# Step order, start and last layer of a seven-layer transformer kernel written as software-pipelined slots

## Time and profile before

| | us |
|---|---|
| three runs | 1559.39, 1562.4, 1566.7 |
| median | 1562.4 |
| the profiled execution's own time | 1564.65 |
| its span in the profile | 1562.9 |
| busy PE / DVE / ACT / POOL in the span | 1311.8 / 892.1 / 893.2 / 354.4 |
| granted TensorE clock, mean | 0.965 |

### The profile page before, as it was taken

The page is one execution under the profiler, slowest core; times in us unless marked ns, Lnnn a source line. Parts: engine busy times, 40 slices in busy tenths (PEclk is TensorE's granted clock), DMA queues, the critical chain, the costliest instruction groups (busy, mean ns, idle before and its releaser), DMA issues.

```text
span 1562.9 us, 66101 instructions
## 1 busy us (share of the span) xinstructions
PE 1311.8 (84%) x29736; PEld 750.4 (48%) x29736; DVE 892.1 (57%) x1825; ACT 893.2 (57%) x1535; POOL 354.4 (23%) x569
## 2 busy tenths in 40 slices
PE   2678889888998888888898988888879888989875
PEld 1344555455555545555554555544534333525333
DVE  3554556554556554555655555554577767787434
ACT  1255666566665666666666666655635565454720
POOL 3123222122223222222221222212211101020212
PEclk8699999999999999999999999999999999999987
DMA  8443344334244333434333434433223222110000
GB/s 164 97 96 83 86 96 91 80 64 95 75 93 110 78 60 84 105 77 98 89 82 70 89 82 88 94 89 51 75 64 59 58 45 61 17 32 4 10 2 15
DMA packets 133775, 113.69 MB, mean 73 GB/s; under 512 B 42360, under 2 KB 121054, under 8 KB 133086
## 3 DMA queue, kind: packets, MB, share of 16 engines
q1 hardware_dynamic: 133494, 109.47, 31.8%
HBM read 62.17 MB, written 47.25 MB: 70 GB/s over the span
## 4 chain that ended last, share of the span: by engine, by line
PE 39%; issue 26%; DVE 18%; POOL 8%; ACT 6%; DMA 3%; SPq 1%; POOLq 0%; DVEq 0%; ACTq 0%
PE pD L742 16%; PE pT L742 7%; PE pV L818 7%; DVE MX L1195 6%; PE pS L759 6%; DVE DEN L1413 4%; PE pD L943 3%; POOL RS L1525 2%; ACT PT L1098 1%; DVE R L1429 1%; ACT SQ L1113 1%; DVE CC L1266 1%; POOL VS L1604 1%; ACT XS L1151 1%; DVE DEN L1406 1%
## 5 line engine op out<-in xcount | busy, mean ns | idle before, releaser
L1098 ACT ACTIVATE PT<-pT 128x512 f32<-128x512 f32 x1088 | 622.6, 596 | 470.3 <-PE pT L742 460.8
L1195 DVE TENSOR_REDUCE MX<-pS 128x1 f32<-128x512 f32 (+4 forms) x928 | 500.2, 573 | 439.5 <-PE pS L759 435.1
L742 PE MATMUL pT<-Qop,Kop 128*32 128x256 bf16 (+2 forms) x7040 | 440.0, 300 | 29.8 <-ACT PT L1098 16.4
L759 PE MATMUL pS<-Kop,Qop 128*32 128x128 bf16 (+4 forms) x7168 | 316.6, 259 | 60.6 <-DVE MX L1195 27.2
L818 PE MATMUL pV<-PT,Vp 128*32 128x256 f32 (+2 forms) x3584 | 315.7, 434 | 5.8 <-ACT PT L1098 5.2
L759 PEld LDWEIGHTS pS<-Kop,Qop 128*32 128x32 bf16 x7168 | 182.0, 98 | 227.0 <-issue 120.7
L742 PEld LDWEIGHTS pT<-Qop,Kop 128*32 128x32 bf16 x7040 | 183.6, 97 | 165.7 <-issue 81.3
L818 PEld LDWEIGHTS pV<-PT,Vp 128*32 128x32 f32 x3584 | 125.2, 110 | 75.1 <-issue 23.1
L1525 POOL TENSOR_TENSOR RS<-VAR,MHALF 128x4 f32<-128x4 f32 x60 | 60.6, 1011 | 415.4 <-DVE VAR L1273 415.4
L1572 POOL TENSOR_TENSOR ATT<-NUM,DEN 128x512 f32<-128x512 f32 x28 | 35.6, 1273 | 407.0 <-DVE DEN L1413 407.0
L742 PE MATMUL pD<-HIDT,W 128*32 128x512 f32 x768 | 104.9, 599 | 0.0
(11 more groups left out here) (178 smaller groups left out, 1385.9 us busy)
## 6 DMA issues: line engine op xcount, KB each, us to landing
Qop<-Qs SPq DMA_DIRECT2D x56, 384.0 KB
Kop<-Ks SPq DMA_DIRECT2D x56, 384.0 KB
Qs<-XS SPq DMA_DIRECT2D x28, 384.0 KB, 2.7
Ks<-XS SPq DMA_DIRECT2D x28, 384.0 KB, 2.9
Qs<-XS SPq DMA_DIRECT2D x28, 256.0 KB, 3.0
Ks<-XS SPq DMA_DIRECT2D x28, 256.0 KB, 3.2
EM<-Es SPq DMA_DIRECT2D x24, 256.0 KB, 3.2
Ms<-MROW SPq DMA_DIRECT2D x336, 4.0 KB, 1.5
```

The costliest lines, as they stand in the source:

```text
L742: ins = matmul(dst[c:min(c + 32, cols)], lhs[:, c:min(c + 32, cols)], rhs, start=start, stop=stop, tile_position=(0, c))
L759: ins = matmul(pS[32 * c:32 * c + 32, k % 2, at:at + w], Qop[:, it.par, h, R * qb:R * (qb + 1)], Kop[:, it.par, h, :] if qb == 0 or it.ful ...
L1098: ac.activation(dst, exp_bank(it, k), ACT.Exp, scale=SCALE).then_inc(t_used, 1)
L1195: ins = ve.tensor_reduce(MX[:, u, g2, qbs[0]:qbs[-1] + 1:step], pS[:, k % 2, at:at + w * len(qbs)].rearrange("p (h n) -> p h n", n=w), axi ...
```

## The change

- Start: x of batch 0, the identity and the position term have a semaphore of their own (x0_in). PE transposes batch 0, then the bias rows, then multiplies Q and K of item 0, and then transposes the others (in pS and pT banks). Q and K of item 1 are multiplied before slot -1 begins. The loads of LOWM, NMQ, SEL, TRI, Wo, W2 and W1 move behind the places of item 1 in SP's slot -1, and are waited for at slot 0.
- EXM moves from step 3 to the start of step 2 on ACT.
- Preparations: centre_wo at step 2 (from 9), DP at PE step 3 and DVE step 4 (from 13 and 14) in pD bank 1 (from bank 0), AP at PE step 3 and DVE step 4 (from 8).
- Full items 25 to 27 ("direct"): no NUM and DEN copies; the reciprocals read PSUM, and DVE multiplies ATT at step 11.
- Halved banks: in items 24 to 26 for every expert product, in item 27 for the odd ones, DVE adds the second half of YE to the first and PE gathers with two products of the identity in place of four.
- Fused closing: DVE computes (x - mean) * G2, then times RS plus H1; POOL adds BE2 to H1 beforehand (residual). NMEAN goes; EPS is added on DVE. The second to last item's closing in the drain stands at steps 12, 16, 28, 30 (from 12, 16, 21, 23).

```diff
-LAST_CLOSE_STEPS = (12, 16, 21, 23)
+LAST_CLOSE_STEPS = (12, 16, 28, 30)
-CONSTS = 7
+CONSTS = 3
+        def direct(it):
+            return it.t > NMASKED
+        def halved(it, i):
+            return it.t < NITEMS - 1 or i % 2 == 1
...
-                + one("DEN", Z is not None, den_done, lambda: Z.t + 1)
+                + one("DEN", Z is not None, rec_done if Z is not None and direct(Z) else den_done, lambda: Z.t + 1)
                 + one("K", A is not None, r1_done, lambda: A.t * 2 + 2)
-                + one("DP", Z is not None and Z.b == 0, dp_done, lambda: Z.l + 1)
...
                 rnd(T, 2)
-                + one("NUM", Z is not None and Z.t < NITEMS - 1, num_done, lambda: Z.t + 1)
+                + one("DP", Z is not None and Z.b == 0, dp_done, lambda: Z.l + 1)
                 + one("AP", A is not None and A.b == 0 and after_norm(A.l), ap_done, lambda: prep_no(A.l))
+                + one("NUM", Z is not None and Z.t < NITEMS - 1, att_done if Z is not None and direct(Z) else num_done,
+                      lambda: Z.t + 1)
...
# SP
-            sp.dma_start(LOWM[:], d["c_lowm"]).then_inc(consts_in, 16)
...
-            load_d(0)
             for sl in slots():
...
                     place(A, 0)
+                if sl.s == -1:
+                    sp.dma_start(LOWM[:], d["c_lowm"]).then_inc(late_in, 16)
...
+                    load_d(0)
                 if B is not None:
                     shift_rows_out(B, 0)
...
# TensorE
-                for e in range(4):
+                for e in range(blocks):
                     ins = mm(bank[:, q * P:(q + 1) * P], IDF[:], YE[:, i % 2, e * P:(e + 1) * P],
-                             start=False, stop=e0 == 1 and e == 3)
+                             start=False, stop=e0 == 1 and e == blocks - 1)
...
+            def project(sl, it, x):
+                bank = bank_for(pe, sl, "K" if x else "Q")
+                mm(bank, (Wk if x else Wq)[:], HT[:, it.b, :], start=True, stop=True).then_inc(qk_filled, 1)
+            first_banks = (pS[:, 0, :], pT[:, 0, :], pT[:, 1, :], pS[:, 1, :])
+            pe.wait_ge(x0_in, 3 * 16)
             for b in range(NB):
+                if b == 1:
+                    pe.wait_ge(rows_in, NROWS_IN * 16 + 16)
+                    mm(pV[:, 0, 0:NCOLS], ROWB[:], IDF[:, 0:NCOLS], start=True, stop=True).then_inc(cols_filled, 1)
+                    pe.wait_ge(ht0_done, 1)
+                    pe.wait_ge(wa_in, 32)
+                    project(Slot(-2), item_at(0), 0)
+                    project(Slot(-2), item_at(0), 1)
+                    pe.wait_ge(x_in, (NB - 1) * 16)
+                transposes(first_banks[b], lambda q: XIN[:, b, q, :], IDF[:], P).then_inc(ht0_filled, 1)
...
             pe.wait_ge(ht0_done, NB)
+            project(Slot(-1), item_at(1), 0)
+            project(Slot(-1), item_at(1), 1)
...
-                    if step == 8 and A is not None and A.b == 0 and after_norm(A.l):
+                    if step == 3 and A is not None and A.b == 0 and after_norm(A.l):
...
-                    if step == 13 and Z is not None and Z.b == 0:
+                    if step == 3 and Z is not None and Z.b == 0:
                         pe.wait_ge(wo_centred, Z.l + 1)
...
# ScalarE (the parts of item 0 and 1 ahead of the slots: first_rows)
+                    if step == 2 and C is not None and not C.full:
+                        act.wait_ge(nm_done, C.t * 2 + 2)
...
-                    if step == 3 and C is not None and not C.full:
...
# VectorE
                 for q in range(QT):
                     ins = ve.bn_aggr(MV[:, q, :], BS[:, q, :])
-                ins.then_inc(ln_st, 1)
+                ch.link(ins)
+                ve.tensor_scalar(VE[:], MV[:, :, 1], EPS, None, ALU.add).then_inc(ln_st, 1)
...
+            def normalise(it):
                 for q in range(QT):
-                    ins = ve.tensor_scalar(XN[:, q, :], x[:, q, :], NMEAN[:, q:q + 1], RS[:, q:q + 1],
-                                           ALU.add, ALU.mult)
+                    ins = ve.scalar_tensor_tensor(out=XN[:, q, :], in0=x[:, q, :], scalar=MV[:, q, 0:1], in1=G2[:],
+                                                  op0=ALU.subtract, op1=ALU.mult)
+                ins.then_inc(ln_xn, 1)
+                dve.wait_ge(ln_xn, it.t - NMASKED + 1)
+                dve.wait_ge(ln_rs, ln_no(it, 0) + 1)
+                dve.wait_ge(hb_done, it.t - NMASKED + 1)
...
+                for q in range(QT):
+                    ins = ve.scalar_tensor_tensor(out=X[:, q, :], in0=XN[:, q, :], scalar=RS[:, q:q + 1], in1=H1[:, q, :],
+                                                  op0=ALU.mult, op1=ALU.add)
+                ins.then_inc(z_done, 1)
...
+                dve.wait_ge(ex_used, n + 1)
+                if halved(it, i):
+                    ve.tensor_tensor(YE[:, i % 2, 0:2 * D], YE[:, i % 2, 0:2 * D], YE[:, i % 2, 2 * D:4 * D], ALU.add) \
+                        .then_inc(ye_done, 1)
...
+                    if step == 11 and Z is not None and direct(Z):
...
+                        ve.tensor_tensor(ATT[:], num_bank(Z), DEN[:], ALU.mult).then_inc(att_done, 1)
-                    if step == 9 and Z is not None and Z.b == 0:
+                    if step == 2 and Z is not None and Z.b == 0:
                         centre_wo(Z.l)
...
# GpSimd
-                gp.tensor_scalar(NMEAN[:], MV[:, :, 0], -1.0, None, ALU.mult)
-                ch.link(gp.tensor_scalar(VE[:], MV[:, :, 1], EPS, None, ALU.add))
                 gp.tensor_tensor(RS[:], VE[:], MHALF[:], ALU.pow).then_inc(ln_rs, 1)
...
-                ch.link(gp.tensor_tensor(X[:], XN[:], rows(G2), ALU.mult))
-                ch.link(gp.tensor_tensor(X[:], X[:], rows(BE2), ALU.add))
+            def residual(it):
                 pool.wait_ge(h1_copied, it.t - NMASKED + 1)
-                return gp.tensor_tensor(X[:], X[:], H1[:], ALU.add)
+                gp.tensor_tensor(H1[:], H1[:], rows(BE2), ALU.add).then_inc(hb_done, 1)
```

More of the change, by code:

```diff
@@ L970, in _ @@
                         ins.then_inc(dp_filled, 1)
+                    if step == 3 and A is not None and A.b == 0 and after_norm(A.l):
+                        pe.wait_ge(wa_in, A.l * 32 + 32)
+                        bank = bank_for(pe, sl, "AP")
+                        mm(bank[:, 0:1], Wq[:], column("be2", A.l - 1), start=True, stop=True)
+                        mm(bank[:, 1:2], Wk[:], column("be2", A.l - 1), start=True, stop=True).then_inc(ap_filled, 1)
+                    if step in (9, 11) and A is not None and sl.s >= 0:
+                        if step == 9:
+                            pe.wait_ge(wa_in, A.l * 32 + 32)
+                            if sl.s >= 2:
+                                pe.wait_ge(xh_done, ht_final(item_at(A.t - NB)))
+                        project(sl, A, 0 if step == 9 else 1)
                     if step == 14 and Z is not None:
@@ L1392, in _ @@
                         scaled(T, 3, HT[:, T.b, :])
-                    if step == 6 and Z is not None:
+                    if step == 4 and A is not None and A.b == 0 and after_norm(A.l):
+                        dve.wait_ge(ap_filled, prep_no(A.l))
+                        bq = col_at("bq", A.l)
+                        ve.tensor_tensor(BQK[:, A.l, :], pD[:, 1, 0:2], COL[:, bq:bq + L + 2:L + 1], ALU.add) \
+                            .then_inc(ap_done, 1)
+                        dve.wait_ge(ap_done, prep_no(A.l))
+                    if step == 4 and Z is not None and Z.b == 0:
+                        l = Z.l
+                        dve.wait_ge(dp_filled, l + 1)
+                        if not Z.full:
+                            ve.tensor_tensor(B1P[:, l, :], pD[:, 1, 1:1 + HID // P], b1[:, l, :], ALU.add)
+                        ve.tensor_tensor(CB1[:, l:l + 1], pD[:, 1, 0:1], CB[:, l:l + 1], ALU.add) \
+                            .then_inc(dp_done, 1)
+                    if step == 6 and Z is not None and not direct(Z):
                         dve.wait_ge(num_filled, Z.t + 1)
@@ L1401, in _ @@
                             ve.tensor_copy(NUM[:], num_bank(Z)).then_inc(num_done, 1)
-                    if step == 8 and Z is not None:
+                    if step == 8 and Z is not None and direct(Z):
+                        dve.wait_ge(den_filled, Z.t + 1)
+                        dve.wait_ge(att_done, Z.t)
+                    if step == 8 and Z is not None and not direct(Z):
                         if not Z.full:
@@ L1422, in _ @@
-                    if step == 9 and Z is not None and Z.b == 0:
-                        centre_wo(Z.l)
-                    if step in (11, 13) and A is not None:
-                        x = 0 if step == 11 else 1
-                        dve.wait_ge(hi_done, A.t * 2 + 1 + x)
-                        if sl.s >= -1:
-                            dve.wait_ge(parts_done, A.t * 2 - 1 + x)
-                        ve.scalar_tensor_tensor(out=R1[:, x, :], in0=pD[:, 1 - x, :], scalar=bias_q(A.l, x),
```

(10 more changed lines are left out.)

165 lines of the change are left out of this document (85 added, 80 removed).

## The result

The changed kernel takes 1511.8 us (median of three, 1506.0 to 1517.5) against 1562.4: ratio 0.969, 95% interval 0.9655 to 0.9725, 50.6 us less. The forecast was 1502, so about 9 us of the 60 did not come. The traced execution took 1517.54 us (span 1515.8), the slowest of its three, while its counterpart took 1564.65.

A forecast was written before the change was run, and what follows sets the result against it. The prediction took TensorE's in-order queue to set the pace, with DVE fuller in the closing stretch. Its terms summed to 60 us, taking 1562.4 to 1502, with a range of 1480 to 1530.

The forecast's parts named there:

- Start: Set-up before slot 0: earlier Q and stores, fewer waits for places; 11.5 us gained, ends 5 and 14.
- Rival (c): At the start, late loads sit in front of the shift rows; 5 us, giving 1507; chance 0.08.
- EXM: Masked slots, ACT's EXM at step 2: 0.35 us in each of 23 slots, 8 us; ends 0 and 18.5.
- rival (a): Masked slots give nothing back, PE stands for NUM's bank and AU instead; 30 of 60 remain, 1532; chance 0.17.
- DP: Wo and W1 preparations moved to steps 2, 3, 4: net 3.0 us in each of six slots, 18 us.
- the last layer's first slot: The same preparation move in that slot, where DVE is the fuller engine: 1.5 us, ends 0 and 3.
- rival (d): Slower: centring at step 2 waits for Wo, W2, W1 and DVE stands before every maximum; 1570 or so; chance 0.02.
- AP: BQK preparation moved from step 8 to 3 and 4: 0.8 us in each of five slots, 4 us; ends 0 and 8.
- Halved banks: Expert gathers lose half their 32 products for one DVE addition each: 7.5 us gained, ends 3 and 10.3.
- Inside the last layer's slots: Direct attention and fused closing inside slots: 2.5 us gained; ends 2 slower and 5 faster.
- rival (b): DVE becomes the last layer's bound, half additions and closing costing what gathers save; 10 us less, 1512; chance 0.1.
- Drain: Final drain: shorter POOL chains, earlier attention and gate steps, plus its gathers' half: 7 us gained, ends 4 and 10.

The follow-up runs named there:

- control: The changed kernel itself, unmodified, measured again as a second set; 1513.8 us (1507.9 to 1520.3), ratio 0.9672.
- rows_later: Changed kernel with the second operand buffer's constant rows issued behind item 0's places instead of in front of its stores; 1511.4 us, ratio 0.9641.
- split_late: dp_split with the late loads also issued only when item 0's shift rows are in the operand; 1511.7 us, ratio 0.9672.
- dp_split: Changed kernel with DP in two parts, Wo's product staying at step 3, W1's 32 products at step 21; 1508.7 us, ratio 0.9637.
- exm_only: Kernel before the change with only EXM's move, step 2 instead of 3 on ACT; 1559.9 us, ratio 0.9965 (0.9946 to 0.9983).
- exm_back: Changed kernel with ACT's EXM put back at step 3; 1511.3 us, ratio 0.968 (0.9634 to 0.9726).
- dp_back: Changed kernel with centring of Wo and DP put back at steps 9, 13 and 14, in bank 0; 1531.5 us, ratio 0.9779.
- dp_wide: Changed kernel with DP's 40 products issued as 10 of 128 columns; 1507.3 us, ratio 0.964 (0.9605 to 0.9674).
- small_wide: Changed kernel with every product of up to 16 result columns issued 128 columns wide; 1545.0 us, ratio 0.9868.

## Why the prediction was right, and where not

The time lies in the range, in the likeliest case, 9 us above its number. Part of that is luck: below, several terms come out at their size for reasons that the forecast did not have. Its statement that the terms' ends reach from 1480 to 1520 is not their sum, which goes from 1470 (93 us gained) to 1542 (20). For the masked slots 2 to 24 the terms make 27 (EXM 8, five of DP's six slots 15, AP 4); the two traces of the changed kernel have 12.9 and 19.1 there. Step by step, forecast and measured:

- **Start**, 11.5: 6.5 (7.6 in control), with the first exponentials of slot 0 at 62.5 and not near 56. The stores went out 4.1 (Q) and 4.4 us (K) earlier, where 6 were expected. Two steps failed. "I take 24" for the places: the stores stood behind the constant rows, 28.6. And "the wait for its places before slot 0 also goes": TensorE's wait of 5.0 us under that name, shown below, is gone, but 2.65 for TRI stand there instead, and item 1's stores still wait for item 0's places, since they use the same buffer; rows_later shows that even 24 would have given nothing. That the seven issues on SP are hidden was right to 0.8 us. Rival (c) occurred in part: split_late, where the loads do not stand in front of the rows, has its first exponentials at 60.3, dp_split at 62.6.
- **EXM**, 8: 5.5 (2.7 to 8.5) by exm_only, less than can be told by exm_back. The price of 0.35 a slot was sound: the 15 plain slots take 44.82 on average in exm_only against 45.10 before, the shortest ones differ by 0.65 to 0.9. That TensorE's holes for code take the difference would be the mechanism of rival (a) with another holder; exm_only suggests it and does not show it.
- **DP**, 18, and the last layer's first slot, 1.5: 14 to 18 together by dp_back. The charge of 0.7 for DVE's additions was 0.74 (3.7 in five), rival (d) did not occur. But the sum was of waits alone, and its credit of 0.5 for centring has no row. Of R's 18.5 us some 5 came back as waits for SQ and PT, which the forecast did not charge, and the clock that TensorE loses behind a stall of 3.75 us, which it did not count, made up for it. The size is right in part by luck.
- **AP**, 4: nothing that can be told. The waits of Q's bank for BQK and for R sum to the same either way.
- **Halved banks**, 7.5: 9.0 by the trace, 6.5 to 8.5 by medians, which alone would not tell it from nothing.
- **Inside the last layer's slots**, 2.5: 2.8 by the trace. DVE is busy 15.09 of 15.44 us in the closing stretch: rival (b) as a bound in that stretch, not as a loss.
- **Drain**, 7: 7.5 (2.45 in front of the gathers, 5.05 behind). XN to the second statistics is 2.4 instead of 5.4, H1T's second pass 0.75 instead of 1.63, so reading that 1.63 as DVE standing for POOL held: POOL's pass, shown below, ran beside it, and with POOL's passes gone the extra time is gone. "Closing under 10 us" is 10.4.

Before (item 1's places, POOL's pass):

```profile
64.93 0.62 PE L759 MATMUL pS<-Kop,Qop 128*32 128x512 bf16 x4 [5.04 <-DMA Qop<-c_zero]
1523.67 1.26 POOL L1535 TENSOR_TENSOR X<-X,H 128x512 f32<-128x512 f32 x1
```

After:

```profile
1483.91 0.75 DVE L1547 SCALAR_TENSOR_TENSOR H1T<-H1T,COL,HT 128x512 f32<-128x512 f32 x1
1506.87 1.12 DVE L1284 SCALAR_TENSOR_TENSOR XN<-pD,MV,G 128x128 f32<-128x128 f32 x4
1509.30 0.87 DVE L1273 BATCH_NORM_STATS2 BS<-X 128x6 f32<-128x128 f32 x4
```

The measured terms sum to 6.5 + 5.5 + 17.5 + 0 + 7.5 + 2.8 + 7.5 = 47, against 50.6 and 53 by the medians; 3 to 6 us of the gain stand in no term. Against the forecast's 60 the terms lack 13: start 5, AP 4, EXM 2.5 and DP 2, less 0.8 in the last layer and the drain. EXM's and AP's shares of this are within what these measurements cannot tell.

## What to carry to other kernels

Before an engine's stall is counted as gain, ask what it will stand for next: of the 18.5 us of waiting for R that DP's move took away, 5 came back as waits for SQ and PT and 3.6 as waits for DP's own additions. Look for the "issue" holes of that engine too; they may take a part, and here their total changes so much between executions (17 to 31 us) that single traces could not settle it. A long stall can also cost clock behind it, so removing it can be worth more than its length. Two waits on the same bank for the same engine may be one; undoing one alone shows it. And where one kernel's executions differ by 15 us, a slot-by-slot comparison of two single traces misleads: the loss in the preparation slots that I first saw was one execution's.

## What was not expected of the hardware

TensorE stood 1 to 4 us for 16 KB of code in a program without branches, 7 times before and 12 after, ending 1.25 to 1.9 us after the packet landed, at places that change between executions. Widening instructions left a total of 8 us, where the changed kernel's masked slots had gone with 17 to 31. That suggests that dense runs of short instructions make it likelier. How code loading and data traffic share the DMA engines was not tried.

Four 32-column products of one result column cost less than one of 128 columns: 0.43 us for 32 in the variance step, 1.05 for the 8 wide ones.

The granted clock fell to its lower level, 1.2 GHz, in preparation slots. In the kernel before and in dp_back it did so mostly at the wait of 3 to 3.8 us for R. In the changed kernel it did so at holes, for instance behind DP's 80 short instructions and, in their midst, 1.61 us of standing for code at 279 (the two stretches are what lies ahead of the fall, and the fall):

```profile
274.00:280.25 6.25, 4.64 (x139) 3.18 (x139) 2.58 (x7) 3.18 (x7) 0.59 (x3) 1.00 0.84 133
280.25:287.08 6.83, 6.03 (x89) 3.07 (x88) 2.71 (x10) 2.04 (x5) 0.00 (x0) 0.50 0.08 13
```

Over all 14 traces, slots 2 to 24, 48 of 57 falls lie inside or just behind a stall of TensorE of 1.4 us or more. Six of the other nine are in dp_wide and small_wide, which have the one-column products in their wide form. The slot at 0.93 has TensorE busy for 42.99 us, the one at 1.00 for 41.22, with the same instructions. Between some kernels the mean clock goes with the time: 0.966 for dp_back, 0.972 for control, 0.975 for dp_split. It is no rule: dp_wide has 0.972 at 1507.3 us, small_wide 0.971 at 1545.0.
